# A fused attention and FFN kernel on one core: GpSimd's low parts moved ahead of Q's decays, FFN activations fetched from another queue, and batch 1's norms at other FFN steps

## What is computed

```python
x = x + _layernorm(attn(_layernorm(x)))
x = x + _layernorm(ffn(_layernorm(x)))

# attn: 32 heads of 128, linear attention with a decay per head
q, k, v = silu(x @ qkv_w.T)             # in blocks of tokens; kv is the running state
scores = (q @ k.T) * diag_decay
out    = scores @ v + (q * q_decay) @ kv
kv     = kv * block_decay + (k * k_decay).T @ v
xf     = out * rsqrt(mean(out * out) + EPS)
attn   = (sigmoid(x @ gate_w.T) * norm_w * xf) @ out_w.T

# ffn: 1792 hidden units, integer weights in {-1, 0, 1} with a scale per row
ffn = (silu(x @ gate_w.T) * (x @ up_w.T)) @ down_w.T
```

## Time and profile before

| | |
|---|---|
| median of 3 runs | 2527.95 us (2527.68 to 2531.14) |
| the profiled execution: its own time | 2525.21 us |
| the profiled execution: span | 2523.4 us |
| TensorE (PE) busy | 2386.4 us, 95% of the span |
| weight loads (PEld) busy | 2022.6 us, 80% |
| VectorE (DVE) busy | 1393.2 us, 55% |
| ScalarE (ACT) busy | 1195.8 us, 47% |
| GpSimd (POOL) busy | 1685.7 us, 67% |
| mean granted TensorE clock | 0.977 |
| moved by DMA | 304.93 MB, mean 121 GB/s |

### The profile page before, as it was taken

One profiled execution on the slowest core, in us unless ns is written; L12 is line 12 of the kernel. 1 busy time (PEld: TensorE's weight loads), 2 busy tenths in 40 slices (PEclk: granted clock), 3 DMA queues, 4 the chain that ended last, 5 costly groups with the idle time before them and its releaser, 6 DMA issues.

```text
span 2523.4 us, 38292 instructions
## 1 busy us (share of the span) xinstructions
PE 2386.4 (95%) x12256; PEld 2022.6 (80%) x12256; DVE 1393.2 (55%) x2479; ACT 1195.8 (47%) x1721; POOL 1685.7 (67%) x1331
## 2 busy tenths in 40 slices
PE   4799999999999999989999999999999998989996
PEld 3688888888888888878888888888888887767775
DVE  5456666656666666545555555555455554544545
ACT  6544444444444444435444445544444443565553
POOL 5577777767777777655777777776677774555564
PEclk7899999999999999999999999999999999989998
DMA  3633333333334333354433433333333335312212
GB/s 113 206 124 121 123 121 121 123 120 123 124 122 124 125 125 125 123 199 138 134 130 128 133 126 126 128 128 114 104 112 112 112 113 176 114 53 73 67 61 90
DMA packets 156935, 304.93 MB, mean 121 GB/s; under 512 B 22464, under 2 KB 88000, under 8 KB 154176
## 3 DMA queue, kind: packets, MB, share of 16 engines
q1 hardware_dynamic: 141744, 275.18, 33.8%
q10 hardware_dynamic: 15120, 28.84, 3.5%
HBM read 216.92 MB, written 87.03 MB: 120 GB/s over the span
## 4 chain that ended last, share of the span: by engine, by line
PE 37%; POOL 19%; DMA 15%; issue 10%; ACT 9%; DVE 6%; SPq 3%; ACTq 0%; DVEq 0%; POOLq 0%
PE proj L1925 22%; PE yp L1925 8%; POOL qd L586 5%; DMA v_tok<-v_blocks 4%; DMA k_blocks<-pd 3%; POOL g_lo L602 3%; DMA k_tok<-k_blocks 3%; POOL sumsq L598 3%; POOL w_odd L571 3%; DMA v_blocks<-vf 2%; DMA nw<-norm_w 2%; PE sc L1991 2%; PE sc L1981 1%; SPq L404 1%; PE sc L1994 1%
## 5 line engine op out<-in xcount | busy, mean ns | idle before, releaser
L1925 PE MATMUL proj<-xb,w_odd 128*128 128x512 f32 x2688 | 709.9, 402 | 39.9 <-ACT g L916 20.8
L1925 PE MATMUL proj<-xb,w_even 128*128 128x512 f32 x2688 | 689.5, 400 | 21.4 <-DMA xb<-x_blocks 6.0
L1925 PEld LDWEIGHTS proj<-xb,w_even 128*128 128x128 f32 x2688 | 501.3, 191 | 129.7 <-issue 11.0
L1925 PEld LDWEIGHTS proj<-xb,w_odd 128*128 128x128 f32 x2688 | 492.4, 190 | 140.4 <-ACT g L916 26.5
L586 POOL TENSOR_TENSOR qd<-q,table 128x512 f32<-128x512 f32 x128 | 164.3, 1295 | 211.4 <-ACT q L932 211.4
L1518 DVE TENSOR_TENSOR g<-sc,g 128x512 f32<-128x512 f32 x128 | 88.4, 690 | 269.0 <-ACT sq L946 269.0
L577 POOL TENSOR_TENSOR ow_lo<-v_tok,ow_hi 128x1024 fp32r<-128x1024 f32 x32 | 76.6, 2394 | 238.5 <-ACT ow_hi L900 238.5
L1925 PE MATMUL proj<-x_t,f_hi 128*128 128x512 f32 x896 | 214.6, 392 | 1.5 <-issue 1.5
L1525 DVE TENSOR_TENSOR y<-yp,y 128x512 f32<-128x512 f32 x240 | 163.1, 680 | 80.4 <-PE yp L1925 79.9
L1925 PE MATMUL yp<-ow_hi,g_hi 128*128 128x512 f32 x512 | 203.5, 397 | 1.3 <-DVE y L1525 1.3
L571 POOL TENSOR_TENSOR w_even<-ws,w_even 128x1024 fp32r<-128x1024 f32 x64 | 153.4, 2397 | 75.0 <-ACT w_even L892 75.0
(11 more groups left out here) (169 smaller groups left out, 4481.8 us busy)
## 6 DMA issues: line engine op xcount, KB each, us to landing
raw<-w_attn SPq DMA_DIRECT2D x128, 512.0 KB, 3.8
k_blocks<-pd SPq DMA_DIRECT2D x64, 512.0 KB, 3.6
k_tok<-k_blocks SPq DMA_DIRECT2D x256, 128.0 KB, 2.9
v_blocks<-vf SPq DMA_DIRECT2D x64, 512.0 KB, 2.7
v_tok<-v_blocks SPq DMA_DIRECT2D x256, 128.0 KB, 2.9
v_tok<-w_out SPq DMA_DIRECT2D x32, 512.0 KB, 3.7
fraw<-w_ints SPq DMA_DIRECT2D x13, 1024.0 KB, 4.9
tile_a<-w_ints ACTq DMA_DIRECT2D x42, 256.0 KB, 3.3
```

The costliest lines, as they stand in the source:

```text
L1925: last = pe.matmul(psum, s, m, start=start and n == 0, stop=n == len(terms) - 1, skip_group_check=more)
```

## The change

Three edits. (1) In every window GpSimd makes the two low parts `gated_lo(a, 1, h)` ahead of three of Q's four decays and one addition of squares. (2) The four loads of `x_t0` move from ScalarE's queue to SyncE's: two behind `v_read(31, 0)`, two behind `v_read(31, 1)`, each still behind its product of G. (3) In the FFN the two roots of `norm_b` stand together behind step 7 (before: behind steps 4 and 5), the norms `normalise_b(2)` and `(3)` behind steps 8 and 10 (before: 5 and 7), the transposes of batch 1's tiles inside steps 10 and 12 (before: behind steps 6 and 8), the root of `norm_c[0]` behind step 17 (before: 16) and its norm behind 18 (before: 17), the root of `norm_c[1]` behind step 20 (before: 18) and its norm behind 21 (before: 19). Steps 20 and 21 leave the loop for that.

```diff
 # GpSimd, window
                 if next_weights:
                     combine_weights(w + 1, KK)
+                gated_lo(a, 1, 0)
+                gated_lo(a, 1, 1)
                 query_decay(w, 0, 1)
                 add_squares(a, 1, 1)
                 query_decay(w, 1, 0)
                 query_decay(w, 1, 1)
-                gated_lo(a, 1, 0)
-                gated_lo(a, 1, 1)
 # SyncE
+            def ffn_activations(s, part, i):
+                sp.wait_ge(proj_done, products_until(STEPS - 1, GG, i))
+                sp.dma_start(x_t0[:, s, part]..., x_t_first[s * CH:(s + 1) * CH, :, part]...)\
+                    .then_inc(x_t_in[s], 16)
 ...
                 if next_weights:
                     weights(w + 1, VV, ...)
+                else:
+                    sp.wait_ge(tile_hi_out, 16 * BT)
+                    sp.wait_ge(tile_lo_out, 16 * BT)
+                    ffn_activations(0, 0, 1)
+                    ffn_activations(0, 1, 6)
                 v_read(w, 1)
+                if not next_weights:
+                    ffn_activations(1, 0, 7)
+                    ffn_activations(1, 1, 2)
 # ScalarE, window 31: the waits and the four load_x_t are gone
-                    act.wait_ge(tile_hi_out, 16 * BT)
-                    act.wait_ge(tile_lo_out, 16 * BT)
 ...
-                    load_x_t(0, 0)
 ...
-                    act.wait_ge(proj_done, products_until(w, GG, 6))
-                    load_x_t(0, 1)
 ...
-                    load_x_t(1, 0)
-                    load_x_t(1, 1)
 # ScalarE, FFN
             numbered_step(4)
             normalise_a(3)
+            numbered_step(5)
+            numbered_step(6)
+            numbered_step(7)
             square_root(norm_b[2])
-            numbered_step(5)
+            square_root(norm_b[3])
+            numbered_step(8)
             normalise_b(2)
-            square_root(norm_b[3])
-            numbered_step(6)
-            mid_hi(2)
-            numbered_step(7)
+            numbered_step(9)
+            numbered_step(10, turn=2)
             normalise_b(3)
-            numbered_step(8)
-            mid_hi(3)
-            for m in range(9, 17):
+            numbered_step(11)
+            numbered_step(12, turn=3)
+            for m in range(13, 18):
                 numbered_step(m)
             square_root(norm_c[0])
-            numbered_step(17)
+            numbered_step(18)
             final_norm(0)
-            numbered_step(18)
+            numbered_step(19)
+            numbered_step(20)
             square_root(norm_c[1])
-            numbered_step(19)
+            numbered_step(21)
             final_norm(1)
 # TensorE, FFN
-                def ffn_step(m, seg):
-                    units(m, 0, seg)
-                    down(m - 1, (0, 1))
-                    units(m, 1, seg)
-                    down(m - 1, (2, 3))
+                def ffn_step(m, seg, turn=None):
+                    for t in range(2):
+                        units(m, t, seg)
+                        if turn is not None:
+                            mid_transposes(turn, (2 * t, 2 * t + 1))
+                        down(m - 1, (2 * t, 2 * t + 1))
```

More of the change, by code:

```diff
@@ L782, in ffn_step @@
                     hidden(m, 1, split=n + 1 if n + 1 < ROUNDS else None, down=n)
-            for m in range(3, 20):
+            for m in range(3, 22):
                 ffn_step(m)
@@ L1209, in normalise_b, with mid_hi @@
                 normalise(y_tile(s), lambda t: xn[:, t], norm_b[s])
-            def mid_hi(s):
-                for t in range(CH):
+            def mid_hi(s, tiles):
+                for t in tiles:
                     tile = (s - 2) * CH + t
@@ L1242, in final_norm, with ffn_step @@
                 normalise(tile, tile, norm_c[s])
-            def ffn_step(m, par, scales=None, convert=None, split=None, down=None):
+            def ffn_step(m, par, scales=None, convert=None, split=None, down=None, turn=None):
                 if scales is not None:
@@ L1756, in statistics_b, with mid_lo @@
                 norm_variances(norm_b[s])
-            def mid_lo(s):
-                for t in range(CH):
+            def mid_lo(s, tiles):
+                for t in tiles:
                     tile = (s - 2) * CH + t
@@ L1806, in statistics_c, with ffn_step @@
                     tile_statistics(lambda t: y2_tile(s, t), norm_c[s], t)
-            def ffn_step(m, d, seg, scales=None, first=False):
+            def ffn_step(m, d, seg, scales=None, first=False, turn=None):
                 if scales is not None:
@@ L1812, in ffn_step, with numbered_step @@
                     hidden(m, t)
+                    if turn is not None:
+                        mid_lo(turn, (2 * t, 2 * t + 1))
                     add_down(d, seg, 2 * t, first)
                     add_down(d, seg, 2 * t + 1, first)
-            def numbered_step(m):
+            def numbered_step(m, turn=None):
                 d = m - 1
                 ffn_step(m, d, 2 * (d // (2 * FG)) + d % 2, scales=m // 2 if m % 2 == 0 else None,
-                         first=d % (2 * FG) < 2)
+                         first=d % (2 * FG) < 2, turn=turn)
             last = STEPS - 1
@@ L1853, in _ @@
             numbered_step(4)
+            numbered_step(5)
             statistics_b(2)
-            numbered_step(5)
-            norm_scales(norm_b[2])
+            numbered_step(6)
             statistics_b(3)
-            numbered_step(6)
-            norm_scales(norm_b[3])
-            mid_lo(2)
             numbered_step(7)
             numbered_step(8)
-            mid_lo(3)
-            for m in range(9, 15):
-                numbered_step(m)
+            norm_scales(norm_b[2])
+            norm_scales(norm_b[3])
+            numbered_step(9)
+            numbered_step(10, turn=2)
+            numbered_step(11)
+            numbered_step(12, turn=3)
+            numbered_step(13)
+            numbered_step(14)
             dve.wait_ge(ds_in, 16)
@@ L1872, in _ @@
             numbered_step(17)
-            norm_scales(norm_c[0])
             statistics_c(1, (0, 1))
             numbered_step(18)
+            norm_scales(norm_c[0])
             statistics_c(1, (2, 3))
             norm_variances(norm_c[1])
-            numbered_step(19)
+            for m in range(19, 22):
+                numbered_step(m)
             norm_scales(norm_c[1])
-            with dve.Fori(FG + 3, ROUNDS - 1) as n:
+            with dve.Fori(FG + 4, ROUNDS - 1) as n:
                 for j in range(2):
@@ L2162, in window, with mid_transposes @@
                 project_out(a, 7)
-            def mid_transposes(s):
-                for t in range(CH):
+            def mid_transposes(s, tiles):
+                for t in tiles:
                     tile = (s - 2) * CH + t
@@ L2257, in ffn @@
                 for m in range(3, 2 * FG):
-                    ffn_step(m, m % 2)
-                    if m == 6:
-                        mid_transposes(2)
-                    if m == 8:
-                        mid_transposes(3)
-                for m in range(2 * FG, 2 * FG + 6):
+                    ffn_step(m, m % 2, {10: 2, 12: 3}.get(m))
+                for m in range(2 * FG, 2 * FG + 8):
                     if m < 2 * FG + 2:
```

25 lines of the change are left out of this document (12 added, 13 removed).

## The result

| | before | after |
|---|---|---|
| median | 2528.11 us (2527.68 to 2531.14) | 2464.21 us (2461.02 to 2467.26) |
| profiled execution: own time, span | 2525.21, 2523.4 us | 2465.49, 2463.7 us |
| TensorE busy | 2386.4 us | 2364.7 us |
| mean granted clock | 0.977 | 0.981 |

Four runs each; the ratio is 0.9743, 95% interval [0.9728, 0.9758]. The change makes the kernel 63.9 us faster by the medians and 59.7 by the two profiled executions.

What follows compares the result with a forecast made beforehand. TensorE, 95% busy at full clock, bounds the kernel, so only its waits and the slow clock behind them count. 37.8 + 6.3 + 6.9 = 51.0 us off the median of 2527.95 gives 2477.0 us, range 2468 to 2497.

Steps and rivals of the forecast that it cites:

- Part 1: Windows: GpSimd's low parts 5.0 us earlier end TensorE's waits and bring V's write forward; gain 37.8 us, bounds 20 to 42.
- next wait: Rival: in most windows another ScalarE or VectorE step is 0.3 to 0.5 us late; about 2495 us, chance 0.17.
- slower: Rival: in the windows Q's decays or K's low parts come late; about 2539 us at 2.0 us each, chance 0.02.
- The small waits for V in some windows: Ordinary windows: might go too with V's earlier write; nothing in the sum, counted only in the upper bound.
- the bound of 42: Upper limit in us for the windows' gain, if small waits for V in some windows go too.
- 26.5 us, the first term: Product 2 of G no longer waits for ScalarE in any window; 26.5 us, from 28 windows.
- 2.2 more: Window 15 into 16: DMA train up to 5.0 us earlier, less 2.8 already counted for window 15's G wait; 2.2 us.
- The 5.7 for window 17's sums of squares: Window 16 into 17: earlier V removes TensorE's 2.25 us wait and 3.4 us of slow clock behind it.
- Part 2: Attention to FFN: activation loads on SyncE's queue gain 7.6 us, less a new 1.3 us wait; 6.3, bounds 3 to 7.6.
- 0.5 x 3.41: Attention to FFN: half of 3.41 us worked at half clock at 2129:2137, counted as gain beside the 5.93 us wait.
- Part 3: FFN steps: waits and slow clock fall from 27.5 to 20.6 us; gain 6.9, bounds 0 to 13.
- the rule behind it: FFN: ScalarE work between an even and next odd step stalls equally long; odd to even, up to 3 us is hidden.

Runs made afterwards that it cites:

- v_held_back: Changed kernel with one more wait on ScalarE, so V is written as late as before the change; ratio to the kernel before 0.9874, span 2481.6 us.
- p2_only: Kernel before with only the four FFN activation loads moved to SyncE's queue; ratio 0.9987, span 2511.8 us.
- p3_only: Kernel before with only the FFN roots, norms and transposes moved; ratio 0.9965, span 2508.3 us.
- no_p2: Changed kernel with the four FFN activation loads back on ScalarE's queue; median 2465.46 us, ratio to the kernel before 0.9776.
- fs_early: Changed kernel with the small load of the first FFN scales issued ahead of the four activation loads on SyncE's queue; median 2465.58 us, ratio 0.9769.
- after_again: The changed kernel run once more, nothing altered; median 2461.99 us, ratio to the kernel before 0.9765.
- p1_only: Kernel before with only GpSimd's low parts moved earlier in every window; ratio 0.9824, span 2472.2 us.
- odd_fs: fs_early with FFN norms behind odd steps, two roots inside step 8 and the last inside step 20; median 2444.32 us, ratio 0.9692.
- The two further moves: odd_fs with the down weights' load behind window 31's output weights, 2447.13 us; that plus one window 15 activation load ahead of V's second read, 2446.31 us.
- half: Changed kernel with the low parts two places later in GpSimd's list, 2.5 us earlier than originally; median 2470.01 us, ratio 0.9792.

## Why the prediction was off

**Part 1: mechanism right, one term left out.** The list order was the cause, the G waits went in all windows, nothing came late in their place (the rivals "next wait" and "slower" are out: intervals of exactly 62.67 us). In the two profiles contributions 1 to 30 gain 49.2 us, where 37.8 were forecast. TensorE does the same matmuls in the same order in both, so the gain can be read off matmul by matmul:

| term of the sum | forecast | before to after |
|---|---|---|
| waits for ScalarE at product 2 of G | 26.5 | 29.1 |
| slow clock behind two of them (windows 17 and 26) | 3.4 | 3.2 |
| waits for VectorE's `k` early in a window | 0 | 6.8 |
| window 15 into 16, up to the product at 1101.74 | 2.2 | 3.1 |
| slow clock behind that product's wait | 0 | 1.6 |
| window 17's sums of squares with their slow clock | 5.7 | 5.7 |
| the rest | 0 | -0.3 |

- The step that failed is the third term. "The small waits for V in some windows" were put at nothing in the sum and stood only in the bound of 42, with no row behind them. VectorE's `turn_v` waits for V and stands ahead of K's combinations, so V's earlier write took 6.8 us of waits for `k` away as well: before's row of 10.1 us in 18 waits went to 3.6 in 2, and 1.5 us more went at the step of K before it. 3.1 of the 6.8 us lie in the two intervals behind contributions 14 and 24. `v_held_back`, whose V is late again, shows the cause. Measured in the same way from `p2_only` and `p3_only` to the changed kernel, this term is 8.9 and 5.6 us.
- "26.5 us, the first term" was right. It is idle time of the weight load; the start of the matmul behind it gave back 28.0, the matmuls right behind that 1.1.
- The transfers, "2.2 more", took 2.8 us off the 5.0 for window 15's own G wait. That one was only 2.0 us, which leaves 3.0, and 3.1 were measured. The product that had waited came 6.7 us earlier: 2.1 for this G wait, 1.5 for waits for `k`, 3.1 for the train. The wait of 5.14 us that the prediction hadn't read is inside this stretch.
- The slow clock behind that wait, 2 x 0.23 x 7.3 = 3.4 us at half speed, cost 1.6 that I had not counted. It is gone in both profiles of the changed kernel, but not in `no_p2` and `fs_early`. This is the row of the kernel before, without which the term can't be seen:

```profile
1101.70:1109.00 7.30, 7.25 (x32) 6.08 (x33) 2.98 (x5) 5.43 (x9) 6.74 (x4) 0.77 0.01 2
```

- The 5.7 for window 17's sums of squares came as forecast, but with luck: in `after_again` they still wait 1.80 us with slow clock behind, and the term is 2.1. That explains its 202.3 us for contributions 14 to 17 against 198.9.

Of the 11.4 us that were missing, the left-out term is 6.8. The profile of before also had longer windows than the two others: the mean gain over all these profiles is 42 us, and `p1_only` has 44 (39 to 49). 42 was no upper bound for part 1.

**Part 2: too large.** Forecast 6.3 us; alone it is 3 (0 to 7), and 2.7 in its stretch (from the contributions of window 30 to the first down product: 100.7 us before, 98.0 in `p2_only`); with part 1 in place it is 0.7. Three steps failed. The wait of 5.93 us for V was counted as if part 1 weren't there, but V's write is 4.5 us earlier with part 1, and `p1_only` has only 2.42 us of that wait left. And the new wait behind was put at 1.3: it is 2.31, as the scales landed 8.8 us after their issue, not 6.0, and the output weights are late on the same queue next. "0.5 x 3.41" for the slow clock was no gain either: from the start of the contributions to the first product of the FFN it was 4.9 us at half clock and is 4.7 at the full one (2078.80 to 2083.53), TensorE now waiting 2.78 us ahead of it where it had waited 1.5. The rule that the prediction named, the Trainium skill, "DMA: Bandwidth & Descriptors", section "Queues, rings and completion order" (one queue's descriptors are consumed in ring order), agrees with `fs_early`: issued ahead of the four loads, the scales wait for nothing.

**Part 3: right in its places, too small in size.** Forecast 6.9; alone it is 9 (5 to 13). In the profile it is 7.7 from step 5 on; the 5.3 us of the table are these less 2.4 lost between the contributions and step 5. (My expectations for the first runs had 6.8 and 1.5 here.) From the first down product to the end it is 342.0 to 347.9 us in seven profiles with these steps and 355.0 to 355.6 in the three with the old ones: 10.0 in the mean. The stalls were 12.7 us, not 13.8, and the slow clock behind the long ones 4.8 in the mean, not 6.8. Stalls at steps 5, 9, 11 and 19 of 2.78 us idle, 3.06 to 3.13 with the start of the matmul, at step 21 1.48 and 1.75 (forecast: four of 2.9 to 3.3 and one of 1.7), none at 6, 7 and 17. `odd_fs` confirms the rule behind it. The drain of 1380 ns that the Trainium skill, "ScalarE: Activation LUTs", section "What ACT_TABLE_LOAD costs", adds to a table load would have made step 21's stall 3.0 us; it isn't seen.

So the stretches sum to 49.2 + 6.1 + 5.3 - 0.9 = 59.7 us. The rest to 63.9 is the spread of the two profiled executions. This result was itself at the high end: run again beside other runs of before, the changed kernel's ratio was 0.9765 [0.9750, 0.9779], about 60 us, and the three parts alone sum to 56.

The best version is the changed kernel with the norms behind odd steps (`odd_fs`, 0.9692), 17.7 us below it. The two further moves add nothing that can be measured.

## What to carry to other kernels

When an early step on one engine frees a wait, follow everything that stands behind that engine in its list: here V's write moved 4.5 us as well, and that was worth 17 us beside the 32 of the wait itself. Look for rows of other waits on the same transfer before leaving them to a bound, and count a stall only once when two parts of a change shorten the same one. Serial work between two steps costs by its place: the same four norms cost 12 us of stall behind even steps and next to nothing behind odd ones. A load put ahead of others on a full queue moved the wait to another place here, twice, and gained nothing that could be measured. And read a small term in more than one profiled execution: here the same windows differed by 6 to 7 us from one to the next.

## What the runs showed of the hardware

The slow clock behind a stall is partly chance. Seven profiled executions (the changed kernel's two, `no_p2`, `fs_early`, `p3_only`, `half`, `v_held_back`) have the same four stalls of 2.8 us at steps 5, 9, 11 and 19. Of these 28, 9 cost nothing behind the stall (the next interval between down products is 5.5 us, as without a stall), 15 cost about 1.5 us (6.9 to 7.2), 4 cost 2.8 to 2.9 (8.4). The same program behind the same stall of step 11: the changed kernel's row 2246:2252 above has a clock of 0.72, `after_again` this one:

```profile
2243.60:2250.00 6.40, 6.37 (x28) 5.33 (x29) 2.69 (x4) 3.30 (x5) 6.00 (x3) 1.00 0.29 82
```

The mean over the 28 is (15 x 1.5 + 4 x 2.85) / 28 = 1.2 us, less than the 1.7 that I counted for each; a single stall can be up to 1.7 us off that mean. Slow clock also stood behind a wait of 1.80 us (`after_again`, 1132 to 1140, clock 0.79) and not behind one of 3.15 (`odd_fs`, 1083 to 1091, clock 1.00). That is why small changes (`fs_early`, `no_p2`) can't be read from a span.
